# A two-layer graph attention on one core: the second layer's values in two fp16 parts, all twelve heads' probabilities turned by DMA, and a new order of the queues

## What is computed

```python
# layer 0: 6 heads of 64
q, k, v = (_heads(x @ W + b) for W, b in ((Wq, bq), (Wk, bk), (Wv, bv)))
probs = softmax(q @ k.T / 8 + where(adj, 0, NEG))
x = layernorm(x + (probs @ v) @ Wf + bf)
# layer 1: 12 heads of 32
h = einsum('bnd,ade->bane', x, W1)
th = tanh(h)
attn = leaky(th @ w_src + swap(th @ w_dst))      # leaky: 0.2 below zero
attn = softmax(where(adj, attn, -999.0))
feat = elu(einsum('banm,bame->bane', attn, h) + b1)
gate = sigmoid(x @ Hw.T + Hb)
x = layernorm(x + gate * feat + (1 - gate) * x)
```

## Time and profile before

| | |
|---|---|
| median of 3 runs | 1194.84 us (1194.11 to 1195.69) |
| profiled execution | 1194.85 us, its span 1192.9 us |
| busy: TensorE (PE) | 1106.4 us, 93% |
| busy: weight loads (PEld) | 1006.0 us, 84% |
| busy: VectorE (DVE) | 988.0 us, 83% |
| busy: ScalarE (ACT) | 918.1 us, 77% |
| busy: GpSimd (POOL) | 937.5 us, 79% |
| mean granted TensorE clock | 0.972 |
| DMA | 90.98 MB, 30.7% of the 16 engines' span |

### The profile page before, as it was taken

One profiled execution on the slowest core, in us unless ns is written; L12 is line 12 of the kernel. 1 busy time (PEld: TensorE's weight loads), 2 busy tenths in 40 slices (PEclk: granted clock), 3 DMA queues, 4 the chain that ended last, 5 costly groups with the idle time before them and its releaser, 6 DMA issues.

```text
span 1192.9 us, 36400 instructions
## 1 busy us (share of the span) xinstructions
PE 1106.4 (93%) x12553; PEld 1006.0 (84%) x12553; DVE 988.0 (83%) x2075; ACT 918.1 (77%) x1803; POOL 937.5 (79%) x813
## 2 busy tenths in 40 slices
PE   4799999999999999999999999999999999999962
PEld 3688988888898888899888889988888998888842
DVE  4577888888888888888888888888898888889863
ACT  4367878778888877887878788887878888787754
POOL 1147888888888888888988888898888889888786
PEclk8899999999999999999999999999999999999975
DMA  4113332233233223323332333333233323323322
GB/s 147 44 37 60 77 92 70 56 91 91 66 81 91 75 53 89 91 70 77 91 79 53 84 91 71 76 91 81 56 79 91 72 74 91 83 58 64 78 64 69
DMA packets 188441, 90.98 MB, mean 76 GB/s; under 512 B 158837, under 2 KB 183418, under 8 KB 188410
## 3 DMA queue, kind: packets, MB, share of 16 engines
q1 hardware_dynamic: 188410, 90.57, 30.7%
HBM read 31.22 MB, written 12.58 MB: 37 GB/s over the span
## 4 chain that ended last, share of the span: by engine, by line
PE 83%; DVE 5%; issue 4%; POOL 3%; ACT 2%; DMA 2%; SPq 1%; ACTq 0%; POOLq 0%; DVEq 0%
PE lin L459 50%; PE zp L556 6%; PE fp L641 5%; PE zp L618 3%; PE zp L614 3%; PE fp L644 3%; PE tp L627 2%; PE tp L593 2%; PE tp L566 2%; PE lin L503 2%; PE tp L498 2%; PE fp L581 2%; DVE ctx_n L1069 2%; DVE p0t_lo L1057 2%; ACT p0t_hi L807 1%
## 5 line engine op out<-in xcount | busy, mean ns | idle before, releaser
L1324 POOL TENSOR_TENSOR z<-z,z_max 128x1536 f32<-128x1536 f32 x64 | 176.3, 2755 | 28.3 <-DVE z_max L1117 24.2
L1336 POOL TENSOR_TENSOR f<-f,x_kept 128x384 f32<-128x384 f32 x64 | 64.3, 1005 | 131.7 <-DVE f L1148 131.7
L1331 POOL TENSOR_TENSOR p_lo<-z,p_hi 128x1024 f16<-128x1024 f32 x64 | 137.5, 2148 | 0.2 <-ACT p_hi L832 0.2
L801 ACT ACTIVATE z<-zp 128x1536 f32<-128x1536 f32 x64 | 93.0, 1453 | 50.6 <-PE zp L618 50.4
L1283 POOL TENSOR_TENSOR prod<-th,w_sd_rows 128x768 f32<-128x768 f32 x64 | 119.2, 1863 | 12.4 <-ACT th L737 8.7
L826 ACT ACTIVATE z<-z,log_scale 128x1536 f32<-128x1536 f32 x64 | 101.8, 1591 | 30.2 <-POOL z L1324 30.2
L792 ACT ACTIVATE p<-p,p_min 128x128 f32<-128x128 f32 x384 | 119.2, 401 | 0.0
L1110 DVE SCALAR_TENSOR_TENSOR z<-zp,z 128x1536 f32<-128x1536 f32 x64 | 111.8, 1748 | 5.5 <-ACT z L801 5.5
L1117 DVE TENSOR_REDUCE z_max<-z 128x12 f32<-128x1536 f32 x64 | 111.5, 1743 | 0.0
L641 PE MATMUL fp<-h_part,p1t_hi 128*128 128x33 bf16 x2304 | 106.1, 178 | 4.5 <-DMA p1t_lo<-p_lo 2.3
L641 PEld LDWEIGHTS fp<-h_part,p1t_hi 128*128 128x128 f16 x2304 | 101.1, 96 | 10.6 <-issue 6.6
(11 more groups left out here) (162 smaller groups left out, 4475.7 us busy)
## 6 DMA issues: line engine op xcount, KB each, us to landing
xt_raw<-x_t SPq DMA_DIRECT2D x32, 384.0 KB, 3.1
x_raw<-x SPq DMA_DIRECT2D x32, 384.0 KB, 3.4
x_kept<-x SPq DMA_DIRECT2D x64, 192.0 KB, 2.4
out<-out_tile SPq DMA_DIRECT2D x64, 192.0 KB, 1.9
adj<-adj SPq DMA_DIRECT2D x64, 32.0 KB, 1.9
dst_row<-sd_t SPq DMA_DIRECT2D x64, 9.0 KB
p1t_hi<-p_hi SPq DMA_TRANSPOSE x64, 3.3
p1t_lo<-p_lo SPq DMA_TRANSPOSE x64, 3.8
```

Source lines behind the costliest of these rows:

```text
L801: act.activation(z[:, g, :], zp[:, :, :].rearrange("p b n -> p (b n)"), ACT.Copy)\
L1324: pool.tensor_tensor(zs, zs, z_max[:, g, :].unsqueeze(2).to_broadcast([128, H1, N]), ALU.subtract)\
L1331: pool.tensor_tensor(p1_lo[:, g, :], z[:, g, PE_HEADS * N:], p1_hi[:, g, :], ALU.subtract).then_inc(w1_lo[g].sem, 1)
```

## The change

1. **Values.** `h` is scaled by `h_scale`, one number worked out at the start from the largest |W1| and |b1|, so that it fits fp16. It is kept in two fp16 parts instead of three bf16 ones. `hidden_part2` (ScalarE) and one GpSimd subtraction go. `attend1` has three matmuls a head instead of five (hi by two parts, lo by the first). The unit is multiplied back in `features_norm`.
2. **Probabilities.** All twelve heads are turned by DMA: `p1_hi`, `p1_lo` and their transposes grow from 8 to 12 heads, and `weights1_transposes`, `turned1_high` and `turned1_low` go. `attend1(g, 0)` now waits for the DMAs; before, only `attend1(g, 1)` did.
3. **Order.** The lists of all five engines and the orders of the PSUM banks are new.

```diff
-PE_HEADS, DMA_HEADS = 4, 8
-LIN_USERS = ("h1", "g0", "qk0", "v0", "pr0", "g1", "pr1", "qk1", "qk2", "v1", "h0")
-TP_USERS = ("pt01", "pt00", "sdt", "pt11", "pt10", "ct0", "ct1", "x1t0", "wt0", "wt1", "x1t1")
+LIN_USERS = ("qk0", "g0", "v0", "pr0", "g1", "pr1", "qk1", "qk2", "v1", "h0", "h1")
+TP_USERS = ("pt01", "pt00", "sdt", "pt10", "pt11", "ct0", "ct1", "x1t0", "x1t1")
-SECOND_BANK = ("g0", "v0", "pr1", "qk2", "h0", "pt01", "sdt", "pt10", "wt0", "x1t1")
+SECOND_BANK = ("g0", "v0", "pr1", "qk2", "h0", "h1", "pt00", "sdt", "pt10", "ct0", "x1t0")
...
                 def attend1(g, k):
                     if k == 0:
                         bank_free(FP_USERS, f"f{g}")
-                        pe.wait_ge(h_done[2][g].sem, prev(h_done[2][g]))
-                        pe.wait_ge(wt_lo[g].sem, now(wt_lo[g]))
-                    if k == 1:
+                        pe.wait_ge(h_done[1][g].sem, prev(h_done[1][g]))
                         pe.wait_ge(wt_turned[g].sem, prev(wt_turned[g]))
...
-                        for i in range(3):
+                        for i in range(2):
                             pe.matmul(o, hi, h_part[i][:, g, h, :], start=(h == 0 and i == 0), stop=False,
                                       skip_group_check=True)
-                        for i in range(2):
-                            last = pe.matmul(o, lo, h_part[i][:, g, h, :], start=False, stop=(i == 1),
-                                             skip_group_check=True)
+                        last = pe.matmul(o, lo, h_part[0][:, g, h, :], start=False, stop=True, skip_group_check=True)
...
+                def hidden_unit():
+                    dve.wait_ge(top_mm.sem, 1)
+                    dve.wait_ge(tops_found.sem, 2)
+                    dve.scalar_tensor_tensor(out=h_unit[:, :], in0=fp[:, D:D + 1], scalar=1.02 * X1_TOP * C,
+                                             in1=b1_max[:, :], op0=ALU.mult, op1=ALU.add).then_inc(unit_made.sem, 1)
...
-                    pool.tensor_tensor(p1_lo[:, g, :], z[:, g, PE_HEADS * N:], p1_hi[:, g, :], ALU.subtract).then_inc(w1_lo[g].sem, 1)
+                    pool.tensor_tensor(p1_lo[:, g, :], z[:, g, :], p1_hi[:, g, :], ALU.subtract).then_inc(w1_lo[g].sem, 1)
```

More of the change, by code:

```diff
@@ L620, in attention1 @@
                     last.then_inc(z_mm[g].sem, 1)
[L622 to L628, removed]
                 def attend1(g, k):
@@ L656, in body @@
                 turn.late(2, attend1, 1, 1)
+                turn.late(1, source_target_transposes)
                 turn.late(2, attend1, 1, 2)
-                turn.step(0, queries_keys, 0)
-                turn.late(1, source_target_transposes)
+                turn.late(0, weights0_transposes, 1, 0)
                 turn.late(0, weights0_transposes, 1, 1)
                 turn.late(0, attend0, 0)
-                turn.late(0, weights0_transposes, 1, 0)
+                turn.late(1, attention1, 0)
                 turn.late(0, context_transposes, 0)
-                turn.late(1, attention1, 0)
                 turn.late(0, attend0, 1)
                 turn.step(0, values, 0)
+                turn.late(0, project, 0)
                 turn.late(0, context_transposes, 1)
-                turn.late(0, project, 0)
                 turn.late(1, attention1, 1)
@@ L674, in body @@
                 turn.step(1, x1_transposes, 0)
-                turn.step(2, weights1_transposes, 0)
                 turn.step(0, values, 1)
@@ L678, in body @@
                 turn.step(1, hidden, 0)
+                turn.step(1, x1_transposes, 1)
                 turn.step(0, scores, 1)
-                turn.step(2, weights1_transposes, 1)
-                turn.step(1, x1_transposes, 1)
+                turn.step(1, hidden, 1)
                 turn.step(2, attend1, 0, 0)
+                turn.step(2, attend1, 0, 1)
             turns(pe, passed, body)
@@ L1118, in z_maxima @@
                                       AX.X, ALU.max).then_inc(z_maxed[g].sem, 1)
-                def turned1_low(g):
-                    dve.wait_ge(wt_hi[g].sem, now(wt_hi[g]))
-                    dve.wait_ge(f_mm[g].sem, prev(f_mm[g]))
-                    dve.tensor_tensor(p1t_lo[:, g, 0:PE_HEADS * N], tp_bank(f"wt{g}")[:, :],
-                                      p1t_hi[:, g, 0:PE_HEADS * N], ALU.subtract).then_inc(wt_lo[g].sem, 1)
                 def features_inverse(g):
@@ L1198, in body @@
                 turn.late(1, z_leak, 0)
-                turn.late(2, stats1, 0)
+                turn.late(1, z_maxima, 0)
+                turn.late(0, add_residual, 0)
                 turn.step(0, value_residue, 0)
                 turn.late(0, context_low, 1)
-                turn.late(0, add_residual, 0)
-                turn.late(1, z_maxima, 0)
                 turn.late(0, stats0, 0)
+                turn.late(0, moments0, 0)
+                turn.late(1, z_leak, 1)
+                turn.late(0, variance0, 0)
@@ L1205, in body @@
+                turn.late(1, z_maxima, 1)
+                turn.late(0, add_residual, 1)
+                turn.late(0, shift_norm0, 0)
+                turn.late(2, stats1, 0)
                 turn.late(2, moments1, 0)
-                turn.late(0, moments0, 0)
+                turn.late(0, stats0, 1)
                 turn.late(2, variance1, 0)
-                turn.late(0, variance0, 0)
-                turn.late(1, z_leak, 1)
-                turn.late(0, add_residual, 1)
-                turn.late(1, z_maxima, 1)
@@ L1233, in body @@
+                turn.step(1, source_target_sums, 0)
+                turn.step(0, scores_min, 1)
                 turn.step(2, features_inverse, 0)
+                turn.late(2, variance1, 1)
+                turn.late(2, shift_norm1, 0)
+                turn.step(2, features_norm, 0)
+                turn.step(1, hidden_raised, 1)
+                turn.step(0, weights0_low, 0, 1)
+                turn.step(0, weights0_low, 0, 0)
+                turn.step(1, source_target_sums, 1)
+                turn.step(2, features_negative, 0)
@@ L1235, in _ @@
+                turn.step(1, source_target_part1)
+                turn.step(1, source_target_residue)
+                turn.late(2, shift_norm1, 1)
+                turn.step(1, source_target_part2)
+                turn.step(1, source_target_part3)
+                turn.step(2, elu, 0)
+                turn.step(2, features_inverse, 1)
+                turn.step(2, features_norm, 1)
+                turn.step(2, features_negative, 1)
             turns(dve, passed, body, other_weights)
```

217 lines of the change are left out of this document (102 added, 115 removed).

## The result

The changed kernel takes **1162.87 us** (median of 4 runs, 1159.72 to 1164.33), the kernel before beside it 1195.26 (1194.11 to 1197.65): a ratio of 0.9723, 95% interval 0.9697 to 0.9749. The forecast was 1186, some 9 us less; it became 32.4 less. The time is that of the first rival (1163), inside the range, but by luck and not for that rival's reason: the DMA does bind.

The account below looks back on a forecast made before the run. Before, TensorE set the 34.68 us turn; afterwards the loop through the 12-head DMA would, at 34.35 (15.5 + 13.7 + 0.1 + 4.4 + 0.65). 1194.85 + 31 x (34.35 - 34.68) + 2 gave 1186 us, range 1158 to 1214.

Parts of the forecast that it names:

- the first rival: The 12-head DMA lands within about 3.6 us, so the products' loop binds at 33.6 us a turn: 1163 us; chance 0.14.
- the landing of the 12-head transpose: Time from the start of issuing graph 1's low-part DMA until its data has arrived: 4.4 us, bounds 3.9 to 4.6.
- the start and the drain: Extra time before the first turn and after the last, taken as 1 us each.
- The lower bound, 3.9: Shortest arrival of the 12-head DMA: issue fixed at 1.24 us, move 2.4, completion 0.3.
- The transposes' loop: Path through GpSimd's `weights1_low(1)`, its DMA and `attend1(1, 0)` to the next `source_target_transposes`: 34.35 us a turn, deciding the time.
- S to Z: From the start of `source_target_transposes` on TensorE to the start of `z_subtract(1)` on GpSimd: 15.5 us.
- from E to Z: From the end of `attend1(1)` through copy, leak and maxima to the start of `z_subtract(1)` on GpSimd: 5.4 us.
- The products' loop: Path through GpSimd's `source_target_products(1)` and VectorE's sums and parts to the next `source_target_transposes`: 33.6 us a turn.
- TensorE's share: TensorE's own work and its new waits for other engines, without the DMA: 33.2 us a turn.
- the hole of the earlier trace: TensorE's 0.97 us idle for `context_norm(0)` before the change, to be hidden by `attention1(0)`.
- The second rival: TensorE's clock falls behind its wait at `attend1(1, 0)`, from about 1.4 us: 1202 to 1233 us; chance 0.26.
- The third: Rival of no difference: both ends meet at 34.55 to 34.75 us a turn; chance 0.12.

Follow-up runs that it names:

- e1: All attention left out, only SBUF-to-SBUF transposing DMAs of 2 to 12 heads timed one at a time: 3.0 us for 8 heads, 3.6 for 12.
- e2: Changed kernel with the second graph's low transpose turning only its last 8 heads (work left out, output off): 1152.71 us.
- e3: Changed kernel with the second graph's low transpose issued as 2 DMAs of six heads, same bytes: 1175.65 us.
- e9: Changed kernel with `source_target_transposes` moved ahead of `attend1(1, 0)` on TensorE: 1178.12 us.
- e8: Changed kernel with the second graph's low transpose issued as 4 DMAs of three heads, same bytes: 1284.12 us.
- e11: Changed kernel with the second graph's low transpose issued as 3 DMAs of four heads, same bytes: 1227.02 us.
- e13: Changed kernel with graph 1's low part made in two pieces on GpSimd, each transposed when ready: 1159.49 us.

## Why the prediction was wrong

**The failed step is the landing of the 12-head transpose**, put at 4.4 us. It is 3.7. 0.7 us too much on a loop that binds, over 31 turns, is 21.7 of the 23 us missed; the start and the drain make up the rest (0.5 us in place of 2), and the other links of the loop cancel to within 0.1 us a turn. Two readings in it were too high and one too low. The issue was taken as growing with the heads "since 1.24 us for one instruction speaks for work by the block"; e1 has 1.2 us before the first packet at 8 and at 12 heads. And the move of 8 heads was read as 1.6 us from a stretch that also held the adjacency load; it is 1.26, so 12 heads take 1.9, not 2.4. What was put at 0.3 for completion is 0.6. In all 1.2 + 1.9 + 0.6 = 3.7. The lower bound, 3.9, was too high as well: it had the issue fixed, but the move was still the one from that window, scaled.

**What held.** The transposes' loop binds: e2 and e3 move the time with the landing, down until the next loop takes over and up one for one. Its other links were right within 0.15 us, S to Z as a whole only: to E it is 10.40 (forecast 10.1), from E to Z 5.18 (5.4). And the chain of work that ended last runs there mostly on VectorE, from `context_inverse(0)` (617.38) to the maxima of graph 1 (630.20), not over TensorE's order and ScalarE's copy, as the sum had it: that copy is done at 626.46, and the leak starts at 626.69, behind VectorE's own small steps. It is this list of VectorE's that e9 ran into. The products' loop is 33.3 (forecast 33.6); of the 0.3 between them, 0.25 lie from the products' end to S, 2.35 in place of 2.6 (which in the earlier trace rows is the time to the end of part 3; S itself came 3.26 behind, when TensorE was free). TensorE's share is 33.1 (33.2). So all three lie within half a microsecond, which fits that no single edit found more than 0.3 us a turn.

**Other steps.** Clock 1.00 in the turns: right, but for the last. The wait at `attend1(1, 0)` is 0.4, not 1.2 us, again the landing. Start and drain were taken as 2 us and came to 0.5. `weights0_transposes(1, 0)` waits 0.32 for the copy of `sd_t` (0.4). `attention1(0)` does hide the norm: the hole of the earlier trace rows is gone.

**Rivals.** The first gave the right time by luck: its condition (landing within 3.6) was just missed, its 33.6 for the products' loop measures 33.3, and its 2 us for start and drain 0.5. The Trainium skill's rule on transposing DMAs (Advanced Engine Details and Errata, X-Bar Transpose (TRN2): as fast as plain ones, 350 to 400 GB/s) is not borne out for these sizes: with nothing else in flight the packets move at 203 GB/s (e1). Its rule that the throttled state is the default and activity releases it (TensorE: Matmul & The Clock Gate, Part 1) agrees with e8, where the clock is at half from some 1 us behind the end of a wait and back at 1.00 by 5 us behind it. The second rival did not occur, but e8 and e11 show its mechanism as described; with a landing of 4.9, as in e11, the change would have been a loss. The third, no difference, did not come.

## What to carry to other kernels

Before a duration is scaled, split it into what comes before the first packet, the move and the completion, in windows of 0.1 to 0.2 us, and look at the queue for a second transfer inside the window; if only one size can be seen, the fixed share is a range of its own. A loop through several engines is added up link by link, and after each edit the next loop has to be added up too: here three of them stood at 33.1, 33.3 and 33.6 us. A step costs only the loops that it stands in: moved past the point from which the next loop counts, it is added to that one, as the 8 heads of e9 were (0.9 us from S to Z).

## What was not expected of the hardware

- An SBUF to SBUF transpose of 128 x 128 fp16 tiles landed after 2.3, 2.4, 2.7, 3.0 and 3.6 us for 2, 4, 6, 8 and 12 tiles (e1).
- TensorE's clock fell to half, between 0 and 2 us behind the end of the wait, behind half of the waits of 1.7 us and all of 2.9 us, and not behind 0.8 us (e3, e8, e11); such a turn cost 1.5 us. Why the wait of 1.7 does it in one turn and not in the next stays open.
- GpSimd's subtract to fp16 took 1.17, 2.14 and 3.13 us for 512, 1024 and 1536 columns (e13): nearly in proportion, with about 0.2 us fixed.
